# Six instead of five of eleven feature tiles by seven block products, in an attention and feed-forward kernel

## The reference

```python
x = x + cross_attention(layernorm(x), ctx, ...)            # x is (8, 1024, 512)
h = layernorm(x)
xq   = fake_quant(h, clip_x)                               # int8 steps, one scale for all of x
gate = einsum('bsh,ih->bsi', xq, weight_quant(w_gate))     # 512 -> 1408 features
up   = einsum('bsh,ih->bsi', xq, weight_quant(w_up))
h    = silu(gate) * up
h    = fake_quant(h, clip_down)                            # one scale: needs max |h| over everything
x    = x + einsum('bsi,hi->bsh', h, weight_quant(w_down))  # 1408 -> 512
```

## Time and profile before

| | us |
|---|---|
| median of three runs | 1243.34 (1241.86 to 1243.46) |
| the profiled execution | 1241.36 |
| its span in the trace | 1239.6 |
| TensorE busy in it | 1231.9 |
| VectorE busy in it | 1046.4 |
| ScalarE busy in it | 849.3 |
| GpSimd busy in it | 362.7 |

### The profile page before, as it was taken

The page is one execution under the profiler, slowest core; times in us unless marked ns, Lnnn a source line. Parts: engine busy times, 40 slices in busy tenths (PEclk is TensorE's granted clock), DMA queues, the critical chain, the costliest instruction groups (busy, mean ns, idle before and its releaser), DMA issues.

```text
span 1239.6 us, 20549 instructions
## 1 busy us (share of the span) xinstructions
PE 1231.9 (99%) x7505; PEld 574.7 (46%) x7505; DVE 1046.4 (84%) x1917; ACT 849.3 (69%) x1331; POOL 362.7 (29%) x283
## 2 busy tenths in 40 slices
PE   8999999999999999999999999999999999999998
PEld 5544444444444444444444444544444444444444
DVE  8977988988898898898898869888888888888777
ACT  7888567657757756765775763467787785499760
POOL 0113343144034124314404420213433332022223
PEclk9999999999999999999999999999999999999999
DMA  8384346255364363362563383499888755199996
GB/s 314 93 253 165 94 139 211 69 173 168 99 180 130 115 214 81 119 222 69 161 212 94 108 235 119 167 264 262 240 256 265 231 153 183 55 357 411 424 426 268
DMA packets 174565, 241.74 MB, mean 195 GB/s; under 512 B 122608, under 2 KB 142080, under 8 KB 156928
## 3 DMA queue, kind: packets, MB, share of 16 engines
q1 hardware_dynamic: 174432, 240.42, 59.8%
q10 hardware_dynamic: 32, 0.01, 0.0%
HBM read 120.86 MB, written 90.57 MB: 171 GB/s over the span
## 4 chain that ended last, share of the span: by engine, by line
PE 92%; DVE 4%; ACT 3%; issue 1%; DMA 0%; SPq 0%; POOL 0%; DVEq 0%; ACTq 0%
PE bank L2436 12%; PE bank L2327 10%; PE po L81 10%; PE po L83 9%; PE po L82 9%; PE ring L83 8%; PE ring L81 8%; PE ring L82 8%; PE bank L2332 4%; PE bank L2333 4%; PE bank L2308 2%; PE bank L2292 2%; PE ring L1256 2%; PE ring L1283 2%; ACT E L479 1%
## 5 line engine op out<-in xcount | busy, mean ns | idle before, releaser
L81 PE MATMUL ring<-yT,M 128*128 128x512 f16 x512 | 194.1, 379 | 0.0
L82 PE MATMUL ring<-yT,M 128*128 128x512 f16 x512 | 194.0, 379 | 0.0
L83 PE MATMUL ring<-yT,M 128*128 128x512 f16 x512 | 194.0, 379 | 0.0
L81 PE MATMUL po<-VW,p 128*128 128x512 f16 x480 | 182.2, 380 | 0.0
L82 PE MATMUL po<-VW,p 128*128 128x512 f16 x480 | 181.9, 379 | 0.0
L83 PE MATMUL po<-VW,p 128*128 128x512 f16 x480 | 181.9, 379 | 0.0
L494 ACT ACTIVATE p<-E 128x512 f16<-128x512 f32 x120 | 74.6, 624 | 122.9 <-DVE E L741 122.9
L417 POOL TENSOR_TENSOR esum<-esum,E 128x512 f32<-128x512 f32 x96 | 129.4, 1348 | 51.3 <-ACT E L483 18.4
L414 POOL TENSOR_TENSOR esum<-E 128x512 f32<-128x512 f32 x16 | 23.4, 1460 | 409.4 <-DVE p L745 369.7
L2436 PE MATMUL bank<-w,hb 128*128 128x512 f16 x605 | 131.2, 379 | 0.2 <-DVE hb L2225 0.2
L1968 ACT ACTIVATE hb<-hb,hscale 128x512 int8<-128x512 f32 (+1 forms) x155 | 95.2, 706 | 17.5 <-DMA hb<-hidden 14.0
(11 more groups left out here) (389 smaller groups left out, 2478.0 us busy)
## 6 DMA issues: line engine op xcount, KB each, us to landing
xa<-x_rows_d SPq DMA_DIRECT2D x28, 1024.0 KB, 7.0
hidden<-hb SPq DMA_DIRECT2D x22, 1024.0 KB, 8.9
hb<-hidden SPq DMA_DIRECT2D x18, 1024.0 KB, 11.1
x<-in_x_dram SPq DMA_DIRECT2D x16, 1024.0 KB, 5.3
value_fold<-E SPq DMA_DIRECT2D x64, 256.0 KB, 2.5
VW<-value_fold SPq DMA_DIRECT2D x16, 1024.0 KB, 5.9
x_rows_d<-x SPq DMA_DIRECT2D x16, 1024.0 KB, 5.3
out_dram<-xa SPq DMA_DIRECT2D x11, 1024.0 KB, 12.1
```

Of the source, the lines that this page charges most:

```text
L81: nc.tensor.matmul(out, a_hi, b_hi, start=first, stop=False)
L82: nc.tensor.matmul(out, a_hi, b_lo, start=False, stop=False)
L83: return nc.tensor.matmul(out, a_lo, b_hi, start=False, stop=last)
```

## The change

`JOINT` becomes 0, 2, 4, 6, 8, 10, so that six tiles of a pair are joint and five single. A pair now starts and ends with a joint tile. The last `joint_close` of a pair is made inside the first round of the next pair, and in the last round the fourth single product stands between `joint_middle` and `joint_late`. ScalarE follows. On VectorE the last `cross` of a pair stands ahead of three of the four `sum_x` of the next pair, and `pair_reach` and `round_x` stand in other places. The weight sums have six tiles instead of five.

```diff
--- before.py
+++ after.py
@@ -1506,7 +1506,7 @@
     LATE = 5
     SEQ_GROUPS = (0, 1, NG - 2, NG - 1)
     PAIRS = range(1, NG // 2 - 1)
-    JOINT = tuple(range(1, FT, 2))
+    JOINT = tuple(range(0, FT, 2))
     NJ, NS = len(JOINT), FT - len(JOINT)
     ALL_J, ALL_S = NJ * len(PAIRS), NS * len(PAIRS)
     joint = lambda p, i: NJ * (p - 1) + i // 2
@@ -1515,10 +1515,10 @@
 
     def count_to(order, what, K):
 
-        before, j, k = K // NJ * NJ * len(order), K % NJ, order.index(what)
+        k = order.index(what)
         if what == order[-1]:
-            return before + (len(order) * (j + 1) + 2 if j + 1 < NJ else NJ * len(order))
-        return before + (len(order) * j + k + (k >= 2) if j > 0 else k + 1)
+            return len(order) * (K + 1) + (2 if K + 1 < ALL_J else 0)
+        return len(order) * K + k + (k >= 2) if K > 0 else k + 1
 
     made_joint = lambda what, K: count_to(PRODUCTS, what, K)
     taken_joint = lambda what, K: count_to(TAKEN, what, K)
@@ -1681,7 +1681,7 @@
             if g // 2 == 2:
                 sp.wait_ge(ups, 2 * FT)
             elif g // 2 > 2:
-                sp.wait_ge(singles, 4 * NS * (g // 2 - 2))
+                sp.wait_ge(joints, made_joint("gate_b", joint(g // 2 - 2, JOINT[-1])))
             for t in range(TT):
                 sp.dma_start_transpose(turned(g)[:, :, t * P:(t + 1) * P], xq_of(g)[:, t]).then_inc(x_turned[g % 2], 16)
 
@@ -1691,8 +1691,8 @@
                 sp.wait_ge(hs, FT * g + m1)
             else:
                 p = g // 2
-                sp.wait_ge(single_hs, 2 * (single(p, (m1 - 1) // 2 * 2) + 1))
-                sp.wait_ge((j_hs_a, j_hs_b)[g % 2], joint(p, (m1 - 2) // 2 * 2 + 1) + 1)
+                sp.wait_ge(single_hs, 2 * (single(p, m1 // 2 * 2 - 1) + 1))
+                sp.wait_ge((j_hs_a, j_hs_b)[g % 2], joint(p, (m1 - 1) // 2 * 2) + 1)
             sp.dma_start(h_d[g][:, m0:m1], hb[:, HOME[g], m0:m1]).then_inc(h_stored[HOME[g]][c], 16)
 
         def load_h(q):
@@ -1750,7 +1750,7 @@
                     store_h(g, c)
         sp.wait_ge(x_turned[(NG - 1) % 2], 64 * (NG // 2))
         load_r(ODD)
-        sp.wait_ge(singles, 4 * ALL_S)
+        sp.wait_ge(joints, made_joint("gate_b", ALL_J - 1))
         load_r(1)
         sp.wait_ge(ups, 4 * FT + 1)
         for slot in range(2):
@@ -1803,7 +1803,7 @@
             pool.wait_ge(ones_set, 2 + DC)
             pool.wait_ge(gate_up_turned, 32)
             pool.wait_ge(x_rounded, 1)
-            every = lambda half, c0: half[:, c0:c0 + 2, P:].rearrange("p c (j u n) -> p c j u n", u=2, n=P)[:, :, :, 0]
+            every = lambda half, c0: half.rearrange("p c (i n) -> p c i n", n=P)[:, c0:c0 + 2, 0:FT:2]
             nc.gpsimd.tensor_tensor(wsum[:, 2], every(wg, 0), every(wu, 0), ALU.subtract).then_inc(w_summed, 1)
             nc.gpsimd.tensor_tensor(wsum[:, 0], every(wu, 0), every(wu, 2), ALU.add).then_inc(w_summed, 1)
             pool.wait_ge(x_rounded, 2)
@@ -1939,25 +1939,26 @@
             if n in (16, 17, 18, 19):
                 normalise_row(4, n - 16)
         for p in PAIRS:
-            single_silu(p, 0, 0)
             for i in JOINT:
                 seed(p, i)
                 keep_third(p, i)
-                single_silu(p, i - 1, 1)
-                if i > 1:
-                    joint_silu_b(p, i - 2)
-                g, t = {1: (2 * p + 3, 0), 3: (2 * p + 3, 2), 7: (2 * p + 4, 0), 9: (2 * p + 4, 2)}.get(i, (NG, 0))
+                if i > 0:
+                    single_silu(p, i - 1, 1)
+                if joint(p, i) > 0:
+                    joint_silu_b(p if i > 0 else p - 1, i - 2 if i > 0 else JOINT[-1])
+                g, t = {2: (2 * p + 3, 0), 4: (2 * p + 3, 2), 6: (2 * p + 4, 0), 8: (2 * p + 4, 2)}.get(i, (NG, 0))
                 if g < NG:
                     normalise_row(g, t)
                 joint_silu_a(p, i)
-                single_silu(p, i + 1, 0)
+                if i < JOINT[-1]:
+                    single_silu(p, i + 1, 0)
                 if g < NG:
                     normalise_row(g, t + 1)
                 keep_fourth(p, i)
-            single_silu(p, FT - 1, 1)
-            joint_silu_b(p, JOINT[-1])
         for n in range(2 * FT, 4 * FT):
             silu(n)
+            if n == 2 * FT:
+                joint_silu_b(PAIRS[-1], JOINT[-1])
         act.wait_ge(scales_ready, 3)
         for q in range(NG):
             slot = h_slot(q)
@@ -2081,7 +2082,7 @@
 
         def pair_reach(p, i):
 
-            if i % 2 == 0:
+            if i not in JOINT:
                 dve.wait_ge(single_hs, 2 * single(p, i) + 2)
             else:
                 dve.wait_ge(j_hs_a, joint(p, i) + 1)
@@ -2111,64 +2112,76 @@
                 round_x(1 + i // 6)
         reach(0, FT - 1)
         join_group(0)
-        for i in range(FT):
+        for i in range(FT - 2):
             hidden(1, i)
-            if 0 < i < 9:
+            if i > 0:
                 reach(1, i - 1)
             if i == 1:
                 round_x(3)
-            if i > 8:
-                sum_x(1, i - 9)
-        sum_x(1, 2)
+        for k in range(3):
+            sum_x(1, k)
+        hidden(1, 9)
+        cross(1, 0)
         sum_x(1, 3)
+        hidden(1, 10)
+        reach(1, 8)
         for p in PAIRS:
             if p - 1 in PAIRS:
+                sum_x(p, 1)
+                single_hidden(p - 1, 9, 1)
+                sum_x(p, 2)
+                sum_x(p, 3)
+                joint_hidden_a(p - 1, 10)
+                cross(p, 0)
+                pair_reach(p - 1, 9)
+                pair_reach(p - 1, 6)
+            single_hidden(p, 1, 0)
+            joint_hidden_a(p, 0)
+            round_x(2 * p + 2)
+            single_hidden(p, 1, 1)
+            cross(p, 2)
+            if p - 1 in PAIRS:
                 pair_reach(p - 1, 8)
-            single_hidden(p, 0, 0)
-            if p - 1 not in PAIRS:
-                reach(1, 8)
-            single_hidden(p, 0, 1)
-            cross(p, 1)
-            if p - 1 in PAIRS:
                 pair_reach(p - 1, 10)
-                pair_reach(p - 1, 9)
+                join_pair(p - 1)
             else:
                 reach(1, 9)
                 reach(1, 10)
                 join_group(1)
-            single_hidden(p, 2, 0)
-            for i in (3, 5, 7):
-                joint_hidden_a(p, i - 2)
-                if i != 5:
-                    round_x(2 * p + 2 + i // 7)
-                single_hidden(p, i - 1, 1)
-                cross(p, i)
-                pair_reach(p, i - 3)
-                pair_reach(p, i - 2)
-                single_hidden(p, i + 1, 0)
-            joint_hidden_a(p, 7)
-            if p - 1 in PAIRS:
-                join_pair(p - 1)
-            pair_reach(p, 6)
-            single_hidden(p, 8, 1)
-            cross(p, 9)
+            single_hidden(p, 3, 0)
+            joint_hidden_a(p, 2)
+            pair_reach(p, 1)
+            single_hidden(p, 3, 1)
+            cross(p, 4)
+            pair_reach(p, 0)
+            single_hidden(p, 5, 0)
+            joint_hidden_a(p, 4)
+            round_x(2 * p + 3)
+            single_hidden(p, 5, 1)
+            cross(p, 6)
+            pair_reach(p, 3)
+            pair_reach(p, 5)
+            single_hidden(p, 7, 0)
+            joint_hidden_a(p, 6)
+            pair_reach(p, 2)
+            single_hidden(p, 7, 1)
+            cross(p, 8)
+            pair_reach(p, 4)
+            single_hidden(p, 9, 0)
+            joint_hidden_a(p, 8)
             if p + 1 in PAIRS:
                 sum_x(p + 1, 0)
-                sum_x(p + 1, 1)
-            single_hidden(p, 10, 0)
             pair_reach(p, 7)
-            joint_hidden_a(p, 9)
-            if p + 1 in PAIRS:
-                sum_x(p + 1, 2)
-            single_hidden(p, 10, 1)
-            if p + 1 in PAIRS:
-                sum_x(p + 1, 3)
+            cross(p, 10)
+        single_hidden(PAIRS[-1], 9, 1)
+        joint_hidden_a(PAIRS[-1], 10)
+        pair_reach(PAIRS[-1], 9)
         for i in range(FT):
-            if i == 1:
+            hidden(2, i)
+            if i == 0:
+                pair_reach(PAIRS[-1], 6)
                 pair_reach(PAIRS[-1], 8)
-                pair_reach(PAIRS[-1], 10)
-            hidden(2, i)
-            if i > 0:
+            else:
                 reach(2, i - 1)
             if i == 1:
                 pair_reach(PAIRS[-1], JOINT[-1])
@@ -2405,25 +2418,27 @@
                 up(s, i)
         for p in PAIRS:
             pe.wait_ge(x_turned[0], 64 * p)
-            single_product(p, 0, 0)
-            single_product(p, 0, 1)
             pe.wait_ge(x_turned[1], 64 * (p + 1))
             for i in JOINT:
                 joint_begin(p, i)
-                single_product(p, i - 1, 2)
-                if i > 1:
-                    joint_close(p, i - 2)
-                single_product(p, i - 1, 3)
+                if i > 0:
+                    single_product(p, i - 1, 2)
+                if joint(p, i) > 0:
```

(15 more changed lines are left out.)

## The result

| | before | after |
|---|---|---|
| median, six runs each (us) | 1242.65 (1241.86 to 1243.74) | 1247.11 (1245.62 to 1247.46) |
| ratio, with its 95% interval | | 1.0036 (1.0025 to 1.0046) |
| profiled execution (us) | 1241.36 | 1247.19 |
| first matmul of pair 1 to first of group 14, in its trace (us) | 215.37 | 218.93 |

A forecast was written before the change was run, and what follows sets the result against it. TensorE's matmul count was taken to bound the pairs. Saving 2.98 us, adding 0.46 entering pair 1 and 6.0 at five pair-to-pair places gave +3.5 us, forecast 1246.8 us, range 1240.6 to 1249.5.

The forecast's parts named there:

- The bound and the saving: In the pairs, TensorE's matmul count sets the time; two fewer per pair save 2.59 us over six pairs.
- The two old waits of 0.2 us: TensorE waits of 0.20 and 0.19 us in two pairs, behind a late VectorE multiplication, claimed to go.
- Inside a pair nothing: Within a pair's rounds, the added ScalarE, VectorE and GpSimd work is hidden and costs nothing.
- Entering pair 1, 0.46 us: At pair 1's start, `second` waits once for ScalarE's copy `seed`: 0.46 us.
- Step (1): Where pair follows pair, `add_fourth` of tile 8 blocks the first sum, delaying `cross` and tile 10's `fourth`: 0.18 us.
- Step (2): Where pair follows pair, GpSimd's `joint_hidden_b` of tile 8 blocks VectorE's second sum; VectorE is free at 0.32 us.
- Step (3): Where pair follows pair, `add_fourth` of tile 10 blocks the third sum, so the new pair's `second` waits 1.03 us.
- The 0.55 us after GpSimd's end: A VectorE sum blocked by GpSimd ends 0.55 us after GpSimd; full 0.69 us would make the total 0.7 higher.
- The sum: Whole kernel: -2.98 saved, +0.46 entering pair 1, +6.0 at five pair-to-pair places, giving +3.5 us.
- VectorE did not win the ports: Rival where pair follows pair: the third sum starts before `add_fourth`; 1242.2 us, no change; chance 0.18.
- the waits did not stay away: Rival where pair follows pair: first sum precedes tile 8's `add_fourth`, no wait to speak of; 1240.8 us; chance 0.15.
- the turned rows were not late: Rival where pair follows pair: transferred rows arrive late, delaying `cross` of tile 10; 1248.5 to 1252 us; chance 0.13.

The follow-up runs named there:

- the run without waits at the five places: Changed kernel with sums moved, first single product before `second`, and group 1's last multiplications before sums entering pair 1; 1239.77 us, the lowest median, 0.9976 of the kernel before.
- the run with the sums moved: Changed kernel with VectorE's second, third and fourth sums of rows and some maxima placed elsewhere, TensorE's order kept; 1240.39 us, 0.9983 of the kernel before.
- The reductions: Changed kernel with the row sums of pairs 3 to 6 replaced by one-operand reductions, output not the reference's; 1241.59 us, 0.9995 of the kernel before.
- the held GpSimd: Changed kernel with GpSimd's `add_fourth` of a pair's last tile waiting for the third sum of the next pair's rows; 1241.82 us, 0.9995 of the kernel before.

## Why the prediction was right

**The bound and the saving.** In the pairs TensorE's count of matmuls sets the time: right. In the run without waits at the five places a pair takes its 164 slots and nothing more, 35.39 us. The two old waits of 0.2 us went as said.

**Inside a pair nothing.** Right: none of the gaps lies inside the rounds, though VectorE is busy for 34 of 36.7 us.

**Entering pair 1, 0.46 us.** Measured 0.55. The place was right, the term 0.09 too small. ScalarE's seed copy of the changed kernel:

```profile
828.26 0.58 ACT L1885 ACTIVATE bank<-bank 128x512 f32<-128x512 f32 x1 [0.67 <-PE bank L2346]
```

TensorE beside it:

```profile
828.22 0.38 PE L2346 MATMUL bank<-hb 128*128 128x512 f16 x1
828.99 0.38 PE L2345 MATMUL bank<-hb 128*128 128x512 f16 x1 [0.39 <-ACT bank L1885]
```

The copy ends at 828.84 and TensorE starts at 828.99, 0.15 us later and not 0.05. I had read 0.05 from a wait for a result in SBUF; this one is in PSUM.

One step beside it failed and had no effect. I had put the end of VectorE's first three sums ahead of pair 1's start. They had to wait for a transfer, which that estimate left out:

```profile
826.50 0.69 DVE L2034 TENSOR_TENSOR hb<-xa 128x1024 f16<-128x1024 f16 x1 [0.83 <-DMA xa<-xq]
```

The third of them ended at 828.52, 0.95 us after the pair's start at 827.57. That is 0.08 us past the slot of `second` (828.44), and only ScalarE's copy, which ended later still, hides it. My mark of 0.46 us over 164 slots for pair 1 was wrong too: its stretch has 162 slots and the 0.27 us at its own `fourth`.

**Step (1), 0.18 us at `fourth`.** Measured 0.26 or 0.27. `cross` started 0.56 us ahead of the due slot, as laid out; the same 0.15 us of release makes the difference (899.02 to 899.17). That the first sum, blocked by `add_fourth`, is enough to cause it is shown by the run in which the sum and the maximum changed places. The run with the sums moved shows the other half: there the sum was blocked as before, and with the maximum out of the way the wait was gone as well. It takes both, the block and a list without room behind it.

**Step (2), the second sum.** Right: `joint_hidden_b` from 898.35, the sum at 898.94, VectorE free at 900.09.

**Step (3), 1.03 us at `second`.** Measured 1.01. GpSimd had the ports 0.22 us before VectorE asked (900.47 and 900.69); I had said 0.29. The reductions and the held GpSimd show that GpSimd's operation at the same moment is the cause, and that neither the list's length nor the seed copy is. That what the two share are ports is no run's finding; for it see the next paragraph.

**The 0.55 us after GpSimd's end.** The rows of the changed kernel have 0.54 to 0.56 again; with the full 0.69 us behind the release the sum would have been 0.7 us higher. The Trainium skill (SBUF — State Buffer, "SBUF: two separate sides") says that whoever starts first has the shared ports for its whole instruction and the other is blocked; it gives no time for the blocked sum's work behind the release. The trace agrees with its rule: the sum that comes 0.22 us late ends after GpSimd's full 1.27 us, and the sum that comes first isn't slowed. Two operands in SBUF are not the only case here: VectorE's rounding, with one, took 1.21 us alone (871.02) and 1.89 where it started 0.47 us into an `add_fourth` (833.35).

**The sum.** Forecast +3.5 us with twelve slots gone. Measured in the traces +4.0 for the same work: 0.38 of old waits and 2.59 for twelve slots go, 6.93 of waits come, where I had 6.5. (The +3.56 between the first and the last line of the pairs looks nearer than it is, since fourteen slots are gone from that stretch.) The medians differ by 4.5 us (3.1 to 5.7), and by 3.6 (2.1 to 5.1) when run again. That 1247.1 came for a forecast of 1246.8 is in part luck: the forecast started from 1243.34, the median of three runs, and the six runs beside the changed kernel have 1242.65, which would have made it 1246.1.

**The rivals.** VectorE did not win the ports, the waits did not stay away, and the turned rows were not late: the waits at all five places are alike within 0.02 us, which a transfer would not give. The rows of the sums show one wait for a transfer, the 0.83 us ahead of pair 1, which in the changed kernel stayed hidden.

## What to carry to other kernels

Where one engine is full, count what a saving on it asks of the others in the places with the least room: the saving of two matmuls per pair was paid for with a deadline for the third sum six slots into the pair, where it had been twenty. Before a VectorE operation with two SBUF operands (or a rounding, as above) is put at a deadline, look at what GpSimd does in that moment; a neighbour on another list can double its duration. And when a wait is taken away, work out when the next operand arrives without it: in two of the runs here it was next in line.

## What the runs showed of the hardware

TensorE starts about 0.15 us after the end of a row that writes PSUM (the seed copy, 828.84 to 828.99; `cross`, 899.02 to 899.17), and 0.05 to 0.07 us after one that writes SBUF (864.06 to 864.11 before; the third sum, 902.28 to 902.34). Why is open.

The first 16 us differ between executions, in work that none of the kernels changes. TensorE in the kernel before:

```profile
6.86 1.70 PE L1325 MATMUL po<-ident 128*128 128x256 bf16 x14
10.22 2.02 PE L1433 MATMUL ring<-ident,E 128*128 128x128 f32 x16 [1.66 <-DVE E L980]
...
12.92 2.81 PE L1353 MATMUL po<-E,M 128*128 128x512 f32 x6
```

And in the changed one:

```profile
8.11 3.17 PE L1325 MATMUL po<-ident 128*128 128x256 bf16 x14
11.27 3.09 PE L1433 MATMUL ring<-ident,E 128*128 128x128 f32 x16
...
15.03 2.38 PE L1353 MATMUL po<-E,M 128*128 128x512 f32 x5
```

Two things add up to the 2.11 us. VectorE's part came 1.05 us later, since the third of four loads of the context landed later. And TensorE's rows took longer: fourteen matmuls of the same shape 3.17 us in place of 1.70 and sixteen others 3.09 in place of 2.02. The longer fourteen cost nothing: in both traces the sixteen start 0.60 us after VectorE's L980 (9.62 and 10.67), which they need. The sixteen cost 1.07.

The clock explains it, though the changed kernel's own trace can't show that. It has no record of the granted clock before 13.62 us, and the view by stretch gives 1.00 where it has none, so its 1.00 says nothing there. The run with GpSimd held back has a record from 4.4 us on. Its fourteen matmuls, columns as above:

```profile
7.89:11.06 3.17, 3.17 (x15) 1.89 (x14) 3.10 (x24) 1.15 (x2) 0.00 (x0) 0.50 0.98 328
```

They too took 3.17 us, at a granted clock of 0.50, the 1.2 GHz level; its sixteen others, at 1.00 again, took 2.02. The kernel before took 1.70 at a recorded 1.00 (6.86 to 8.56). In the changed kernel run again the record has 0.50 from 8.2 to 15.1 us, and the sixteen took 3.67. The f32 products began there at 15.38, in the fastest variant at 15.62 (no record before 14.5 us), in others at 13.0 to 13.9. Since the fastest variant is among the late ones, it is not tied to the change, but one or two traces of each don't tell how often. The medians differ by 4.5 and by 3.6 us where the pairs with the two matmuls behind them give 4.0; how much of that comes from the start stays open.
